# Last mixture-of-experts layer: one of two knobs on how many row scatters GpSimd lets be in flight

## What is computed

```python
x = _layernorm(x + linear_attention(x))           # layer 0
x = _layernorm(x + moe_32_experts_top4(x))        # layer 0
x = _layernorm(x + mamba(x))                      # layer 1, a selective scan
x = _layernorm(x + moe_8_experts_top2(x))         # layer 1, the last stage

# the last stage, per token
scores = softmax(xf @ gate_w.T); _, idx = top_k(scores + gate_b, 2)
h  = silu((xf @ w1[e] + b1[e]) * (xf @ w3[e] + b3[e]))     # H = 176, D = 128
y  = sum over the two chosen experts of scores[e] * (h @ w2[e] + b2[e])
z  = the same with one shared expert (sw1, sw3, sw2), for every token
out = _layernorm(x + y + z)
```

## Time and profile before

| what | us |
|---|---|
| median of 3 runs | 2035.29 |
| the 3 runs | 2023.69, 2035.29, 2036.34 |
| the profiled execution, its own time | 2016.17 |
| the profiled execution, from first to last instruction (span) | 2014.5 |
| the last stage in it | from about 1440 to 2014.5 |
| first and last scatter issued | 1464.3 and 1668.2 |
| last shared-expert addition (L1694) | 1636.1 |

### The profile page before, as it was taken

One profiled execution on the slowest core, in us unless ns is written; L12 is line 12 of the kernel. 1 busy time (PEld: TensorE's weight loads), 2 busy tenths in 40 slices (PEclk: granted clock), 3 DMA queues, 4 the chain that ended last, 5 costly groups with the idle time before them and its releaser, 6 DMA issues.

```text
span 2014.5 us, 23835 instructions
## 1 busy us (share of the span) xinstructions
PE 1505.1 (75%) x6020; PEld 913.1 (45%) x6020; DVE 1397.4 (69%) x2668; ACT 977.2 (49%) x1676; POOL 1375.4 (68%) x962
## 2 busy tenths in 40 slices
PE   5777753426989988889998888997687549787681
PEld 3665643312344433334443334443364348676571
DVE  3999971112999999999999999999635332255453
ACT  2444430104566556666555666655334236555450
POOL 2444454754999999999999999989365641354644
PEclk8788865557899999899998989999888779889895
DMA  5222249433322222332222333232213127667562
GB/s 152 87 82 82 82 124 235 63 43 116 116 100 76 100 99 111 121 121 92 82 79 109 121 121 112 62 118 99 58 42 109 49 85 212 197 198 217 173 198 73
DMA packets 214095, 227.65 MB, mean 113 GB/s; under 512 B 24072, under 2 KB 181704, under 8 KB 209736
## 3 DMA queue, kind: packets, MB, share of 16 engines
q1 hardware_dynamic: 191240, 201.12, 30.9%
q0 software_dynamic: 22784, 25.71, 6.4%
HBM read 167.32 MB, written 61.90 MB: 114 GB/s over the span
## 4 chain that ended last, share of the span: by engine, by line
PE 35%; DVE 24%; issue 16%; another core or an unknown queue 8%; POOL 6%; ACT 4%; DMA 4%; SPq 2%; DVEq 1%; POOLq 0%; ACTq 0%
PE bank L1272 11%; DVE hst L1644 11%; PE bank L1227 5%; DVE prod L1660 2%; POOL dbx L778 2%; PE bank L1091 1%; PE bank L1363 1%; PE bank L1376 1%; PE bank L1360 1%; PE bank L1225 1%; DMA wv<-packed_weights 1%; PE bank L1239 1%; PE bank L1261 1%; PE bank L1285 1%
## 5 line engine op out<-in xcount | busy, mean ns | idle before, releaser
L778 POOL TENSOR_TENSOR dbx<-u,ball 128x1024 f32<-128x1024 f32 x256 | 615.3, 2514 | 4.8 <-POOL u L809 2.8
L1644 DVE TENSOR_TENSOR_SCAN hst<-bank,dbx 128x512 f32<-128x512 f32 x512 | 591.7, 1204 | 8.2 <-ACT bank L983 4.0
L1272 PE MATMUL bank<-prod,ident 128*128 128x512 f32 x1024 | 516.9, 642 | 19.2 <-DVE prod L1660 15.2
L983 ACT ACTIVATE bank<-dt,aneg 128x511 f32<-128x511 f32 x512 | 346.3, 687 | 276.1 <-DVE hst L1644 273.5
L1272 PEld LDWEIGHTS bank<-prod,ident 128*128 128x128 f32 x1024 | 208.4, 206 | 261.9 <-issue 211.4
L1660 DVE TENSOR_TENSOR prod<-hst,bank 128x1024 f32<-128x1024 f32 x192 | 233.5, 1216 | 17.2 <-DVE hst L1644 13.8
L840 POOL DMA_INDIRECT yg<-expert_rows,row_of x128 | 123.4, 964 | 132.9 <-DMA expert_rows<-yu 85.4
L787 POOL TENSOR_TENSOR prod<-hst,call 128x1024 f32<-128x1024 f32 x64 | 162.5, 2539 | 26.9 <-DVE hst L1644 26.8
L1683 DVE SCALAR_TENSOR_TENSOR hg<-bank,wv,ha 128x256 f32<-128x256 f32 x96 | 42.0, 479 | 183.3 <-ACT ha L1036 150.6
L1256 PE MATMUL bank<-parts,sel_c 128*128 128x512 bf16 x192 | 76.4, 399 | 73.6 <-DVE prod L1660 72.9
L828 POOL DMA_INDIRECT sorted_rows<-x3b,row_of x80 | 76.6, 957 | 61.4 <-issue 21.7
(11 more groups left out here) (286 smaller groups left out, 3012.2 us busy)
## 6 DMA issues: line engine op xcount, KB each, us to landing
ball<-b_rows SPq DMA_DIRECT2D x32, 2048.0 KB, 7.1
wv<-packed_weights SPq DMA_DIRECT2D x96, 322.0 KB
call<-b_rows SPq DMA_DIRECT2D x16, 1024.0 KB, 9.4
xr<-sorted_rows SPq DMA_DIRECT2D x48, 256.0 KB
expert_rows<-yu SPq DMA_DIRECT2D x48, 256.0 KB
xg_rows<-xg SPq DMA_DIRECT2D x16, 320.0 KB, 3.0
xt<-in_x SPq DMA_DIRECT2D x16, 256.0 KB, 3.2
xT<-in_xT SPq DMA_DIRECT2D x16, 256.0 KB, 3.6
```

The lines of the kernel that those rows point to most:

```text
L778: gp.tensor_tensor(dbx[n % NDB][:, :, :], u[s.par][:, :, :], ball[:, n:n + 1, :].to_broadcast([P, NH, SEQ]), ALU.mult).then_inc(dbx_rdy, 1)
L983: act.activation(da_ps[h][:, 1:SEQ], dt_[s.par][:, h, 1:SEQ], ACT.Exp, scale=aneg[:, h, n:n + 1]).then_inc(da_rdy, 1)
L1272: last = mm(y_ps[:, h, :], ident[:, :], from_[:, h, :], start=False, stop=(n == NS - 1), skip_group_check=True)
L1644: dve.tensor_tensor_scan(h_of[:, h, :], da_ps[h][:, :], dbx[n % NDB][:, h, :], 0.0, ALU.mult, ALU.add).then_inc(scan_rdy, 1)
```

## The change

The constant becomes one for each batch, and batch 0 gets 1 in place of 4; batches 1, 2 and 3 keep 4:

```diff
-PAUSE = 4
+PAUSE = (1, 4, 4, 4)
...
             def send_rows(b):
                 gp.wait_ge(route1, b * ROUTE + 32)
                 for i, k in enumerate(range(first_seq[b] * TT, (last_seq[b] + 1) * TT)):
-                    if i and i % PAUSE == 0:
+                    if i and i % PAUSE[b] == 0:
                         gp.wait_ge(sent[b], 2 * i * 16)
                     for c in range(2):
                         gp.indirect_dma_start(xs_d[b][:, :], bass.IndirectOffsetOnAxis(row_of[:, c, k:k + 1], 0), x3_tile(k), None
```

## The result

| | before | changed |
|---|---|---|
| median of 3 runs, us | 2035.29 | 2005.07 |
| the runs | 2023.69 to 2036.34 | 2004.83 to 2008.49 |
| profiled execution, own time / span | 2016.17 / 2014.5 | 2004.83 / 2003.2 |

The ratio is 0.9879 (95% interval 0.9848 to 0.9910): faster by 1.2%. The forecast was 2023 with a range of 2000 to 2043. The profiled execution became 11.3 us shorter, where the sum said 12.

What follows compares the result with a forecast made beforehand. The prediction took the shared expert to be bound by PE's late handovers beside long scatter runs. It summed -17.9 given back, +6 still lost and 0 direct cost to -12 us, so 2035.29 becomes 2023, range 2000 to 2043.

Steps and rivals of the forecast that it cites:

- What bounds the stage: Shared expert beside POOL's scatters: it waits for PE's late handovers, later the longer the run; 9.6 us a step against 6.6.
- The cost on POOL and SP: Batch 0: 18 more waits of 1.26 us, 22.7 us, covered by POOL's idle times and SP's slack; direct cost 0.
- rival C: Beside batch 0: loss goes by the time scatters are under way, landings don't clear it; 2042 to 2055 us, chance 0.17.
- The loss beside pairs: Batch 0's stretch: 48 scatters at 0.12 us each still lose 6 us, against 17.9 us lost before.
- rival A: Batch 0's stretch: the waits clear the lateness fully, loss goes to 0; 2017 us, perhaps 2007; chance 0.20.
- The straight line: Scatters of POOL: loss each grows by 0.05 to 0.07 us a unit of run length, giving 0.12 for runs of 2.
- The later batches: Batches 1 to 3 keep their long runs and losses of 16.9 and 29.1 us; a step or two moves to first units.
- a sign of being wrong: Between 1624 and the end: batch 0's gain given back by the units that now meet batch 2's scatters.
- The sum: Profiled execution: -17.9 + 6 + 0 = -12 us, 2016.17 to 2004; the same 12 off the median gives 2023.
- the 69 us ahead of the gathers: POOL: the gathers come 69 us behind batch 3's scatters, so its delay was not expected to reach them.

Runs made afterwards that it cites:

- the kernel with fours: Changed kernel with batches 1 to 3 in runs of 4 scatters in place of 8, batch 0 in pairs, late chip: 1962.11 us, ratio 0.9663.
- the repeat: The changed kernel once more on a late chip, against the kernel before at 2029.17 us: 2009.7 us, ratio 0.9898.

## Why the prediction was right, and where it was not

**What bounds the stage.** Right for the kind of chip that the trace came from. The shared expert waited for PE's handovers, and up to the first gather these were late all but only beside scatters in long runs. Shown by the step times beside pairs and fours on late chips, where nothing but the stops differs. On quick chips nothing waits so, which the trace of before couldn't tell. One reading was off: "the last two took 17.7 and 24.6 us" is of the two steps before the last. The last took 5.0 us, up to 1636.14, with POOL idle from 1633; that speaks for the same mechanism.

**The cost on POOL and SP.** Right in each figure: 1.56 us in most gaps ahead of a pair, batch 1 without idle time, SP's first load at 1552.31, 15.4 us ahead of the last shared addition even though this came 68 us sooner. That the waits cost the end nothing holds here because the units' results came late enough to leave POOL's program its slack (see on rival C).

**The loss beside pairs.** I took 6 us, from a loss that grows with the run (0.54 us a scatter at 8, 0.91 at 16). It is about 0, which was rival A: the six steps took 38.3 us, and 38.2 on a quick chip where nothing is late. So this stretch gave back 19.1 us in place of 12. The straight line was the wrong shape: runs of 4 lose next to nothing as well.

**The later batches.** This is the step that failed: "their losses of 16.9 and 29.1 us stay", and only "a step or two" of the harm lands on the first units, "at about the same price a scatter". Nothing was put into the sum for it. In fact the shared expert, freed beside the pairs, was done 17 us after batch 0's last scatter and met only 17 us of runs of 8 in place of 155, so it gained 64 us in place of 12. Of the 80 scatters of batches 1 to 3, 68 then fell on the units: 98.6 us from the last shared addition to the fourth unit's result, where the kernel with fours needed 27.1 on a chip of the same kind (1562.70 to 1589.76). And their price rose. That kernel took 81 us from the seventh addition to the fourth unit's result. Against this, the 80 scatters behind batch 0 cost 61 us before, 0.76 each, and 76 after, 0.95 each. The missing term is these 15.4 us, which took back most of the 19.1. The prediction had named this as a sign of being wrong: the gain "given back between 1624 and the end, by the units that now meet the scatters of batch 2". It came so, from 1568 on.

Why the price rose is argued from the rows, and two causes fit. Before, POOL's idle times of 14 and 15 us at 1531 and 1633 gave the chain a rest; after, batches 1 to 3 went on for 111 us without one, and the units' steps grew to 32.5 us. I had counted these idle times only as cover. But with the second of them gone, batch 2 also meets batch 3 without a stop, which makes a second run of 16 scatters, from 1631 to 1652, and the step of 32.5 us lies beside it. No run removed the idle times alone.

**The sum.** -11.3 against -12, made of -19.1 and +15.4 in the stretch and -7.7 outside it, in place of -17.9 and +6. That is luck: by the mechanism alone the two traces differ by 3.6 us, and the trace of the repeat by 0.4. The median moved by 30 us, or 25 by the ratio: the changed runs spread over 3.7 us and the runs before over 12.7, and the profiled execution of before was the quickest of its kernel. The forecast's own range, 2010 to 2032, was too narrow at its lower end; the full range held.

**Rival C.** It did not happen as told (lateness carried through the pairs). What a stretched batch 0 can cost is another thing, which the prediction had put at nothing on the strength of POOL's idle times: POOL's program as the bound. It is real on the quick chips: 10 us for a batch 0 drawn out by a filler, 78 us for pairs everywhere. I had counted the 69 us ahead of the gathers as slack. They were slack only because the units were late.

## What to carry to other kernels

Time won at one place is worth what the next place lets through: follow it to the first point where both traces stand still together, here the end of the scatters at 1662 and the fourth unit. Slack that a stall has made is not slack, and a wait that cures the stall will spend it; so before putting waits on an engine, count what stands behind it on its program once everything else is on time. And where an unchanged kernel differs by 8% and more between chips, a result belongs to the kind of chip: pairs in batch 0 with fours behind it gained 3.4% on a late one, and no version here was shown to be better on both kinds.

## What the runs showed of the hardware

- The same program has PE's semaphores arrive on time on some chips and late on others, while POOL issues indirect DMAs in runs of 8: with pairs in all batches, ACT's "remote" waits beside the gathers are 79.4 us on a late chip and 0 on two quick ones. In the changed kernel on a late chip, PE's hidden product of the third unit stands at 1628.09, and ACT's instruction that waits for it at 1653.70:

```profile
1628.09 1.03 PE L1376 MATMUL bank<-xu,wv 128*128 128x256 f32 x4
```
```profile
1653.70 0.84 ACT L1036 ACTIVATE ha<-bank,wv 128x256 f32<-128x256 f32 x2 [17.07 <-remote]
```

- The traces of late chips also lack records. Batch 1's 40 scatters count 16 each, 640 in all; counted in the traces of late chips are 147 (before), 106 and 109 (changed, two chips), 272 (fours) and 568 (pairs), and 634 to 640 on every quick chip. So late chips are those that lose records of semaphore updates; but the two don't go together in full, since the kernel with fours lost over half of these records and its units were on time. Whether the recording makes the handovers late, or both have one cause, is open: every timed run has its span and clock recorded, and there was none without recording to compare.
- A stop for landing is no constant: 1.26 us over the plain gap in most cases beside the shared expert (1.4 on average), and on average 2.3 us over it (2.6 less 0.30) in batches 1 to 3, mostly beside the units' loads. The Trainium skill has a fixed cost of some 2.0 us a DMA ("DMA: Bandwidth & Descriptors", "Anatomy of one DMA — SWDGE (gpsimd) path"); the idle gap behind a pair, which is not quite the same thing, lay on either side of that, at 1.56 us and at 2.6 on average.
